# An expert phase dissolved into the attention heads around it, and the expert sums added in the last 20 heads

## The chip, the cores and the metric

One core of one Trainium2 chip. The metric is the device time of one execution in microseconds (us); the figure of a kernel is the median of its runs.

## The reference, cut to what matters

The input x is (4, 1024, 256). One layer norm feeds both an attention and a mixture of experts; both results are added to x.

```python
xn = _layernorm(x)                         # 4096 tokens, 256 columns
x = x + attention(xn) + moe(xn)
# attention: 16 heads of 128, causal softmax over 1024 tokens, @ Wo + bo
# moe:
shared = silu(g_s) * y_s @ w_shared_down   # y_s, g_s = split(xn @ w_shared_up)
scores = sigmoid(xn @ w_gate)              # 64 experts, top 6, weights normed
up  = einsum('ecd,edh->ech', x_disp, w_up) # x_disp: 128 token places an expert
g_r, v_r = split(up)                       # 32 hidden columns each
out_r = einsum('ech,ehd->ecd', silu(g_r) * v_r, w_down)
routed = (out_r[flat_e, pos_c] * w).sum(over the 6 chosen)
```

## The kernel before, in words

There are 64 heads: 4 batch rows times 16 heads, numbered 0 to 63 and worked one after the other. Each engine has its own order, written out by hand in a function `attention(i0, i1)` (one each for SP L401, POOL L530, PE L741, ACT L934 and DVE L1357), and semaphores tie the orders together. In a head, eight blocks of 128 query rows (j = 0 to 7) go through: PE `scores` (L697) into four PSUM banks; DVE `block_max` (L1307), which moves them to SBUF with the row maximum; ACT `softmax_exp` (L865) and `high_probs` (L870), POOL `low_probs` (L483), which split the exponentials into two f16 halves; SP `transpose_probs` (L387), a transposing DMA; and PE `values` (L712) and `project_y` (L727), one head behind the scores. `add_y` (L1330) on DVE adds a head's output to `resid`, the running sum. Queries, keys and values of the next head (`project_q`, `project_k`, `project_v`) are cut into the order between blocks; they and their readers `high_*` (ACT) and `low_*` (DVE) use the two banks of `ps_t`. `ps_y` holds the output of `project_y`. Block 0 to 7 of a head is also called slot 0 to 7 here.

The mixture of experts has four parts:

- Routing. In heads 0 to 32 the gates, the shared expert and the slots of the chosen experts are worked out, in even, odd and late parts of heads (`even_part`, `odd_part`, `late_part`). In heads 2 to 33 POOL scatters normed rows to a DRAM table `dispatched` with indirect DMAs (`scatter`, L511).
- Experts. After head 33 (`SPLIT` = 34) every engine leaves `attention`, with the last head's values and outputs finished and no new head begun. Then `experts(g, first)` runs 8 rounds of two groups of four experts (L806 on PE). A group loads 512 rows (`ex`), turns them to columns with 8 PE transposes (L816) into the score banks, which ACT (L1017) and DVE (L1475) copy to `exT`; runs 8 up projections (L826) of 64 columns; works out the silu with ACT (L1022) and four DVE instructions (L1480 to L1486); transposes the hidden rows (L832), which ACT copies (L1026); runs four down projections (L838) of 32 rows and 256 columns, each pair of halves of `eo` copied by ACT (L1034) and DVE; and stores `eo` to `expert_out` (L1040). All of it is f32. When all stores have landed, a new `attention(34, 64)` starts with its projections.
- Gathers. From head 34 on, POOL gathers one row tile per indirect DMA (`gather`, L522, called in L530's order after `low_probs`) into `got`: 32 token tiles times 6 choices. The order gives one step a slot, 7 steps to a token tile, of which 6 gather.
- Mixes. DVE `mix` (L1345) adds `got` times its weight to `resid` (L1352), and once a tile the constant `cvec` (L1355): 7 steps a tile, 224 in all, one a slot, 12 slots (`MIX_LAG`) behind the gathers, so 8 a head to slot 3 of head 63. `mix_at(j)` is called after block 1 for slots 0 and 1, between the two `low_q` for slot 2, after block 3 for slots 3 and 4, after block 5 for slots 5 and 6, and after block 7 for slot 7.

## Time and profile before

| | us |
|---|---|
| median of 3 runs (lowest, highest) | 1820.65 (1816.66, 1821.87) |
| profiled execution, its own time | 1822.72 |
| its span, first to last instruction | 1821.0 |
| PE busy | 1690.2 (93%) |
| DVE busy | 1368.7 (75%) |
| POOL busy | 1122.1 (62%) |
| ACT busy | 1085.7 (60%) |

Busy time is the union of an engine's instructions; PE's ends are modelled, so a busy PE can still run below its peak. PEclk is the clock that was granted to TensorE, as a share of 2.4 GHz. In the page's 40 slices of the span the four of the expert phase and of the stop around it (21 to 24) have PE busy 8, 6, 7 and 7 tenths and a granted clock of 9, 7, 6 and 6; in most others both have 9.

### The profile page before, as it was taken

How to read it: one execution, taken by the hardware profiler on the slowest of the kernel's cores; microseconds unless marked ns; L12 is line 12 of the kernel's file. 1: busy time of each engine (PE TensorE's matmuls, PEld its weight loads, DVE VectorE, ACT ScalarE, POOL GpSimd, SP SyncE). 2: the span in 40 equal slices, each digit the busy share in tenths (PEclk: the TensorE clock that was granted, in tenths of full speed). 3: DMA queues.
4: the chain of work that ended last, by engine and by line, in shares of the span. 5: the costliest groups of instructions: out<-in, count | busy, mean ns of one | idle time of the engine just before them, and what ended most of it. 6: DMA issues, size and time to landing. Idle time of an engine off the chain costs nothing. (4 is left out here: it accounts for less than half of the span.)

```text
span 1821.0 us, 49686 instructions
## 1 busy us (share of the span) xinstructions
PE 1690.2 (93%) x19217; PEld 1315.9 (72%) x19217; DVE 1368.7 (75%) x3128; ACT 1085.7 (60%) x2347; POOL 1122.1 (62%) x1006
## 2 busy tenths in 40 slices
PE   4699999999999999999986779999998999999997
PEld 3477767777777777777665667777776777777775
DVE  8677777777677777777663446888888888888885
ACT  2566666665566666666661227666666666666664
POOL 0257757776676777776660006777777677777763
PEclk7799999999999999999997669999999999999998
DMA  9377667765656665656656656778988789898976
GB/s 372 112 152 131 121 120 128 135 112 101 120 94 101 96 106 95 96 95 101 115 99 160 206 160 119 138 142 141 164 140 159 122 141 165 139 143 136 163 129 113
DMA packets 686658, 245.04 MB, mean 135 GB/s; under 512 B 637456, under 2 KB 674721, under 8 KB 685536
## 3 DMA queue, kind: packets, MB, share of 16 engines
q1 hardware_dynamic: 657472, 197.83, 61.6%
q0 software_dynamic: 18432, 33.64, 7.7%
q10 hardware_dynamic: 10528, 10.49, 1.8%
q8 instruction: 150, 2.46, 0.5%
q14 instruction: 76, 0.62, 0.1%
HBM read 57.11 MB, written 50.46 MB: 59 GB/s over the span
## 5 line engine op out<-in xcount | busy, mean ns | idle before, releaser
L485 POOL TENSOR_TENSOR prob<-prob 128x128 f16<-128x128 f32 (+7 forms) x512 | 653.0, 1280 | 576.1 <-ACT prob L874 569.2
L867 ACT ACTIVATE prob<-prob,nmax 128x128 f32<-128x128 f32 (+7 forms) x512 | 396.8, 775 | 530.4 <-DVE prob L1312 514.3
L708 PE MATMUL ps_s<-kT,qT 128*128 128x512 f16 (+3 forms) x2304 | 459.7, 327 | 4.3 <-DVE prob L1312 4.3
L723 PE MATMUL ps_o<-probT,vh 128*128 128x256 f16 (+1 forms) x3840 | 428.3, 265 | 7.2 <-DMA probT<-prob 7.2
L1312 DVE TENSOR_SCALAR_CACHE_REDUCE prob<-ps_s,neg_scale 128x128 f32<-128x128 f32 (+7 forms) x512 | 412.2, 809 | 14.3 <-PE ps_s L710 10.6
L723 PEld LDWEIGHTS ps_o<-probT,vh 128*128 128x128 f16 x3840 | 368.7, 99 | 53.5 <-issue 9.1
L874 ACT CAST prob<-prob 128x128 f16<-128x128 f32 (+7 forms) x512 | 341.5, 667 | 2.3
L708 PEld LDWEIGHTS ps_s<-kT,qT 128*128 128x128 f16 x2304 | 201.9, 98 | 144.7 <-issue 4.3
L1341 DVE SCALAR_TENSOR_TENSOR resid<-ps_y,yscale,resid 128x256 f32<-128x256 f32 x512 | 223.0, 477 | 11.6 <-PE ps_y L737 5.8
L737 PE MATMUL ps_y<-wo,oT 128*128 128x256 f16 x1536 | 210.6, 273 | 22.2 <-DVE oT L1327 20.4
L599 PEld LDWEIGHTS ps_t<-xT,wq 128*128 128x128 f16 x6144 | 205.1, 100 | 24.6 <-issue 9.8
L525 POOL DMA_INDIRECT got<-expert_out,slot_idx x192 | 201.1, 1048 | 32.6 <-issue 28.5
L599 PE MATMUL ps_t<-xT,wq 128*128 128x64 f16 x6144 | 214.3, 196 | 4.2 <-issue 2.3
L518 POOL DMA_INDIRECT dispatched<-xn,slot_idx x192 | 192.6, 1003 | 33.5 <-issue 33.0
L622 PE MATMUL ps_t<-xT,wk 128*128 128x512 f16 x768 | 189.2, 383 | 4.1 <-DVE qT L1293 4.0
L643 PE MATMUL ps_t<-wv,xT 128*128 128x128 f16 x3072 | 183.6, 220 | 9.6 <-DVE wv L1141 9.0
L1327 DVE SCALAR_TENSOR_TENSOR oT<-ps_o,oT 128x256 f16<-128x256 f32 x256 | 107.5, 420 | 109.6 <-ACT oT L898 106.0
L643 PEld LDWEIGHTS ps_t<-wv,xT 128*128 128x128 f16 x3072 | 175.7, 98 | 17.6 <-DVE wv L1141 9.3
L737 PEld LDWEIGHTS ps_y<-wo,oT 128*128 128x128 f16 x1536 | 138.7, 98 | 47.1 <-DVE oT L1327 27.2
L1299 DVE SCALAR_TENSOR_TENSOR kT<-ps_t,bkT,kT 128x512 f16<-128x512 f32 x128 | 95.8, 749 | 94.3 <-ACT kT L878 86.0
L1352 DVE SCALAR_TENSOR_TENSOR resid<-got,gate_w,resid 128x256 f32<-128x256 f32 x192 | 148.3, 772 | 3.2
L1293 DVE TENSOR_TENSOR qT<-ps_t,qT 128x512 f16<-128x512 f32 x128 | 87.8, 688 | 59.2 <-ACT qT L886 51.7
(182 smaller groups left out, 1651.6 us busy)
## 6 DMA issues: line engine op xcount, KB each, us to landing
dispatched<-zeros SPq DMA_DIRECT2D x16, 512.0 KB, 14.1
probT<-prob SPq DMA_TRANSPOSE x512
ex<-dispatched SPq DMA_DIRECT2D x16, 512.0 KB, 4.3
expert_out<-eo ACTq DMA_DIRECT2D x16, 512.0 KB, 3.7
eup<-in_L_ffn_w_up_dram SPq DMA_DIRECT2D x64, 64.0 KB, 2.1
dispatched<-xn,slot_idx POOLq DMA_INDIRECT x192
xn_columns<-xnth SPq DMA_DIRECT2D x24, 128.0 KB
got<-expert_out,slot_idx POOLq DMA_INDIRECT x192
```

The costliest lines, as they stand in the source:

```text
L485: pool.tensor_tensor(low_cols(j), prob_cols(j).rearrange("p (r k) -> p r k", k=P), high_cols(j), ALU.subtract).then_inc(p_low, 1)
L518: pool.indirect_dma_start(out=disp_d, out_offset=bass.IndirectOffsetOnAxis(ap=slot_idx[:, t, k:k + 1], axis=0), in_=xn[:, t // 2 % 3, t % ...
L525: pool.indirect_dma_start(out=got[:, t % 2, k, :], out_offset=None, in_=eout_d, in_offset=bass.IndirectOffsetOnAxis(ap=slot_idx[:, t, k:k ...
L599: mm = pe.matmul(ps_t[:, half, col:col + TPH], wq[:, a, k, m * D:(m + 1) * D], xT[:, c, k, h * TPH:(h + 1) * TPH], start=False, stop=(n + ...
L643: mm = pe.matmul(ps_t[:, half, r * D:(r + 1) * D], xT[:, a, k, tok:tok + P], wv[:, c, k, h * D:(h + 1) * D], start=(n + k == 0), stop=(n + ...
L708: pe.matmul(s_cols(j, lo, hi), qT[:, u, a, j * P:(j + 1) * P], kT[:, u, c, lo:hi], start=(n == 0), stop=(n == 2 and hi < w))
L723: mm = pe.matmul(ps_o[:, lo:2 * P], vh[:, u, a, r * D:(r + 1) * D], probT[:, PT_AT[c] + 2 * r + s, lo:], start=(r + n == 0), stop=(r == 2 ...
L737: mm = pe.matmul(ps_y[:, e * C:(e + 1) * C], oT[:, c % 2, a, e * P:(e + 1) * P], wo[:, s, h, :], start=(n == 0), stop=(n == 2))
L867: nc.scalar.activation(prob_cols(j), prob_cols(j), ACT.Exp, bias=nmax[:, j:j + 1], scale=-1.0, accum_out=rsum[:, i % 2, j:j + 1]).then_inc ...
L874: nc.scalar.copy(high_cols(j), prob_cols(j).rearrange("p (r k) -> p r k", k=P)).then_inc(p_high, 1)
L1312: V.tensor_scalar(prob_cols(j), s_cols(j, 0, (j + 1) * P), neg_scale[:], None, ALU.mult, ALU.min, accum_out=nmax[:, j:j + 1]).then_inc(s_m ...
L1341: ins = V.scalar_tensor_tensor(out=row, in0=ps_y[:, e * C:(e + 1) * C], scalar=yscale[:, j:j + 1], in1=row, op0=ALU.mult, op1=ALU.add)
```

## The change

The loop `experts` and the split of `attention` are gone; every engine runs heads 0 to 63 in one order. Head i of 35 to 42 is `early` for groups 2e and 2e+1 (e = i - 35): their rows are turned to columns and group 2e is projected up. Head i of 36 to 43 is `later` for groups 2e-2 and 2e-1 (e = i - 35): group 2e-1 is projected up, both are projected down, copied and stored. The four row blocks of a group go through `ps_t[0]` and `ps_y` in the place of the score banks; `exT`, `eup`, `edn` and `eo` are single instead of double. The hidden values are first copied from PSUM to SBUF (`eu`, ACT) and DVE reads them there. The down projection is two matmuls of 64 rows and 512 columns, with `edn` zero where the experts don't meet, in the place of four of 32 rows and 256 columns. The loads of rows move from SP to ACT, the stores are cut in two, and the loads of weights stay on SP, between the transposing DMAs. Gathers start in head 44 (`GA0`), after the last store has landed; mixes run at 12 a head (`MIXES`), 10 slots behind: one in slots 0, 2, 4 and 6 and two in slots 1, 3, 5 and 7, to slot 7 of head 63.

```diff
-        MIX_LAG = 12
+        MIX_LAG = 10
+        MIXES = 12
         NP = NT // 2
         ROWS = 2 * NP
-        SPLIT = ROWS + 2
+        NGR = E // EG
+        EX0 = ROWS + 3
+        GA0 = EX0 + NGR // 2 + 1
         GATES = E + 2 * HS
...
+        def early(i):
+            return i - EX0 if EX0 <= i < EX0 + NGR // 2 else -1
+
+        def later(i):
+            return i - EX0 if EX0 < i <= EX0 + NGR // 2 else -1
+
+        def gathers_by(s):
+            return max(0, min(NT * TOPK, s * MIXES * TOPK // (TB * (TOPK + 1))))
+
+        def mixes_by(s):
+            return max(0, min(NT * (TOPK + 1), (s - MIX_LAG) * MIXES // TB))
...
+            def load_up(n):
+                if n:
+                    sp.wait_ge(eu_done, n)
+                else:
+                    sp.wait_ge(ex_in[0], 16)
+                for e in range(EG):
+                    sp.dma_start(eup[:, e, :, :], w_up[n * EG + e].rearrange("(k p) n -> p k n", p=P)).then_inc(eup_in, 16)
+
+            def load_down(n):
+                if n:
+                    sp.wait_ge(ed_done, 2 * n)
+                else:
+                    sp.wait_ge(edn_zero, 1)
+                for e in range(EG):
+                    sp.dma_start(edn[e * HE:(e + 1) * HE, e % 2 * C:(e % 2 + 1) * C], w_down[n * EG + e]).then_inc(edn_in, 16)
...
-
-            attention(0, SPLIT)
-
-            for n in range(6):
-                sp.wait_ge(scattered[n], 16 * TOPK * len(range(n, NT, 6)))
-            sp.wait_ge(y_added, NC * SPLIT)
...
-            load_experts(0, True)
-            with sp.Fori(1, E // EG // 2) as g:
-                load_experts(g, False)
-            attention(SPLIT, B * H)
+                        if j == 0 and early(i) >= 0:
+                            load_up(2 * early(i))
+                        if j == 0 and later(i) >= 0:
+                            load_down(2 * later(i) - 2)
+                        if j == 3 and later(i) >= 0:
+                            load_down(2 * later(i) - 1)
+                        if j == 4 and early(i) >= 0:
+                            load_up(2 * early(i) + 1)
+
+            attention(0, B * H)
...
+            for i in range(B * H):
...
+                    if i == EX0 and j == 0:
+                        pool.wait_ge(ex_in[0], 16)
+                        pool.memset(edn[:], 0.0).then_inc(edn_zero, 1)
+                    s = TB * (i - GA0) + j
+                    for n in range(gathers_by(s), gathers_by(s + 1)):
+                        gather(n)
...
+            def rows_to_columns(i, n, h):
+                dst = ps_t[:, 0, :] if n % 2 + h == 0 else ps_y[:]
+                if n % 2 + h:
+                    pe.wait_ge(y_added, NC * (i - 1) + 2 * (n % 2) + h + 1)
+                elif turn(i, True):
+                    pe.wait_ge(v_low, 2 * i + 1)
+                else:
+                    pe.wait_ge(q_low, 2 * i + 3)
+                if h == 0:
+                    pe.wait_ge(ex_in[n % 2], 16 * (n // 2 + 1))
+                for e in range(2):
+                    for k in range(KC):
+                        mm = pe.transpose(dst[:, (2 * e + k) * P:(2 * e + k + 1) * P], ex[:, n % 2, 2 * h + e, k * P:(k + 1) * P], ident[:])
+                mm.then_inc(et_done, 1)
+
+            def up_project(i, n):
+                if n % 2:
+                    pe.wait_ge(y_added, NC * (i - 1) + 1)
+                elif n:
+                    pe.wait_ge(eo_d, n - 1)
+                else:
+                    free_bank(i, 1)
+                pe.wait_ge(eup_in, 16 * EG * (n + 1))
+                pe.wait_ge(eta_ready, n + 1)
+                pe.wait_ge(etd_ready, n + 1)
+                dst = ps_y[:, 2 * P:] if n % 2 else ps_t[:, 1, 2 * P:]
+                for e in range(EG):
+                    for k in range(KC):
+                        mm = pe.matmul(dst[:, e * 2 * HE:(e + 1) * 2 * HE], exT[:, e, k, :], eup[:, e, k, :],
+                                       start=(k == 0), stop=(k == KC - 1))
+                mm.then_inc(eu_done, 1)
+
+            def hidden_columns(i, n):
+                pe.wait_ge(eh_ready, n + 1)
+                if n % 2:
+                    pe.wait_ge(eo_d, n)
+                else:
+                    pe.wait_ge(y_added, NC * (i - 1) + 1)
+                dst = ps_t[:, 1, 0:P] if n % 2 else ps_y[:, 0:P]
+                pe.transpose(dst, eh.rearrange("p e h -> p (e h)"), ident[:]).then_inc(eht_done, 1)
+            def down_project(i, n, h):
+                bank = (n + h) % 2
+                if n % 2 == 0:
+                    free_bank(i, bank)
+                elif h == 0:
+                    pe.wait_ge(eu_taken, min(n + 2, NGR))
+                else:
+                    pe.wait_ge(k_low, 2 * (i + 1) + 1)
+                if h == 0:
+                    pe.wait_ge(edn_in, 16 * EG * (n + 1))
+                    pe.wait_ge(eht_ready, n + 1)
+                two = slice(2 * h * HE, 2 * (h + 1) * HE)
+                pe.matmul(ps_t[:, bank, :], ehT[two, n % 2, :], edn[two, :], start=True, stop=True).then_inc(ed_done, 1)
...
+                if c == 0 and early(i) >= 0:
+                    pe.wait_ge(etd_ready, 2 * early(i) + 2)
+                if c == 1 and later(i + 1) >= 0:
+                    pe.wait_ge(eht_ready, 2 * later(i + 1) - 1)
+                    pe.wait_ge(eu_taken, 2 * later(i + 1))
+                if c == 2 and early(i + 1) >= 0:
+                    pe.wait_ge(etd_ready, 2 * early(i + 1) + 1)
+                if c == 3 and early(i + 1) >= 0:
+                    pe.wait_ge(eta_ready, 2 * early(i + 1) + 2)
...
+                    if later(i) >= 0:
+                        hidden_columns(i, 2 * later(i) - 2)
+                        up_project(i, 2 * later(i) - 1)
...
+                    if early(i) >= 0:
+                        rows_to_columns(i, 2 * early(i), 0)
+                    if old:
                         values(i - 1, 2)
                     scores(i, 3)
+                    if early(i) >= 0:
+                        rows_to_columns(i, 2 * early(i), 1)
...
+                    if later(i) >= 0:
+                        down_project(i, 2 * later(i) - 2, 0)
+                        down_project(i, 2 * later(i) - 2, 1)
+                    if old:
...
+                    if later(i) >= 0:
+                        hidden_columns(i, 2 * later(i) - 1)
+                    if early(i) >= 0:
+                        up_project(i, 2 * early(i))
+                        rows_to_columns(i, 2 * early(i) + 1, 0)
...
+                    if later(i) >= 0:
+                        down_project(i, 2 * later(i) - 1, 0)
...
+                    if early(i) >= 0:
+                        rows_to_columns(i, 2 * early(i) + 1, 1)
+                    if later(i) >= 0:
+                        down_project(i, 2 * later(i) - 1, 1)
...
-            attention(0, SPLIT)
-            pe.wait_ge(y_added, NC * SPLIT)
-            def experts(g, first):
...
-            experts(0, True)
-            with pe.Fori(1, E // EG // 2) as g:
-                experts(g, False)
-            pe.wait_ge(eo_a, E // EG)
-            pe.wait_ge(eo_d, E // EG)
-            attention(SPLIT, B * H)
+            attention(0, B * H)
...
+            def load_expert_rows(n):
...
+                    act.wait_ge(et_done, 2 * n - 2)
+                act.dma_start(ex[:, n % 2, :, :], rows_v[n]).then_inc(ex_in[n % 2], 16)
...
+            def first_columns(n):
+                act.wait_ge(et_done, 2 * n + 1)
+                if n:
+                    act.wait_ge(eu_done, n)
+                nc.scalar.copy(exT[:, 0:2, :, :].rearrange("p e k s -> p (e k s)"), ps_y[:] if n % 2 else ps_t[:, 0, :]).then_inc(eta_ready, 1)
+            def take_hidden(n):
+                act.wait_ge(eu_done, n + 1)
...
+                src = ps_y[:, 2 * P:] if n % 2 else ps_t[:, 1, 2 * P:]
+                nc.scalar.copy(eu[:].rearrange("p e n -> p (e n)"), src).then_inc(eu_taken, 1)
+            def gate_of_hidden(n):
+                act.wait_ge(eu_taken, n + 1)
+                nc.scalar.activation(eg, eu[:, :, 0:HE], ACT.Exp, scale=-1.0).then_inc(eg_exp, 1)
+            def copy_hidden(n):
+                act.wait_ge(eht_done, n + 1)
...
+                src = ps_t[:, 1, 0:P] if n % 2 else ps_y[:, 0:P]
+                nc.scalar.copy(ehT[:, n % 2, :], src).then_inc(eht_ready, 1)
+            def first_outputs(n):
+                act.wait_ge(ed_done, 2 * n + 1)
...
+                nc.scalar.copy(eo[:, 0:2, :].rearrange("p e c -> p (e c)"), ps_t[:, n % 2, :]).then_inc(eo_a, 1)
+
+            def store_outputs(n, h):
+                act.wait_ge(eo_d if h else eo_a, n + 1)
+                act.dma_start(outs_v[n][:, 2 * h:2 * h + 2, :], eo[:, 2 * h:2 * h + 2, :]).then_inc(eo_out[h], 16)
...
+            def second_columns(n):
...
+                V.tensor_copy(exT[:, 2:4, :, :].rearrange("p e k s -> p (e k s)"), ps_y[:]).then_inc(etd_ready, 1)
+
+            def hidden(n):
+                dve.wait_ge(eg_exp, n + 1)
+                V.tensor_scalar(eg, eg, 1.0, None, ALU.add).then_inc(eh_step, 1)
...
+                V.reciprocal(eh, eg).then_inc(eh_step, 1)
...
+                V.tensor_tensor(eg, eu[:, :, 0:HE], eh, ALU.mult).then_inc(eh_step, 1)
+                dve.wait_ge(eh_step, 3 * n + 3)
+                V.tensor_tensor(eh, eu[:, :, HE:], eg, ALU.mult).then_inc(eh_ready, 1)
+            def second_outputs(n):
+                dve.wait_ge(ed_done, 2 * n + 2)
...
+                V.tensor_copy(eo[:, 2:4, :].rearrange("p e c -> p (e c)"), ps_t[:, (n + 1) % 2, :]).then_inc(eo_d, 1)
...
                     def mix_at(j):
-                        n = TB * (i - i0) + j - MIX_LAG
-                        if mixing and 0 <= n < NT * (TOPK + 1):
+                        s = TB * (i - GA0) + j
+                        for n in range(mixes_by(s), mixes_by(s + 1)):
                             mix(n // (TOPK + 1), n % (TOPK + 1), NC * (i - 1) + (1, 1, 1, 2, 2, 3, 3, 4)[j])
...
+                    if later(i) >= 0:
+                        hidden(2 * later(i) - 1)
+                    if i == EX0 - 1:
+                        gate_weights()
...
+                    if early(i) >= 0:
+                        second_columns(2 * early(i))
...
+                    if later(i) >= 0:
+                        second_outputs(2 * later(i) - 2)
...
+                    if early(i) >= 0:
+                        hidden(2 * early(i))
...
+                    if early(i) >= 0:
+                        second_columns(2 * early(i) + 1)
+                    if later(i) >= 0:
+                        second_outputs(2 * later(i) - 1)
                     mix_at(7)
...
-            attention(0, SPLIT, False)
...
```

## Rows read from the trace of the kernel before

**Rows 1.** ACT timeline (start, duration): first exponential of heads 36, 45, 46.
```profile
1138.69 0.40 ACT L867 ACTIVATE prob<-prob,nmax 128x128 f32<-128x128 f32 x1
...
1350.65 0.40 ACT L867 ACTIVATE prob<-prob,nmax 128x128 f32<-128x128 f32 x1
...
1374.22 0.40 ACT L867 ACTIVATE prob<-prob,nmax 128x128 f32<-128x128 f32 x1
```

**Rows 2.** stretches: length, busy us by engine, clock, DMA share, GB/s.
```profile
931.80:1138.70 206.90, 164.85 (x1411) 135.19 (x1412) 102.50 (x224) 75.62 (x169) 51.22 (x45) 0.78 0.63 154
...
1061.00:1074.00 13.00, 9.68 (x66) 8.41 (x66) 6.25 (x13) 3.43 (x8) 0.00 (x0) 0.76 0.74 221
...
1350.60:1374.20 23.60, 23.53 (x294) 18.37 (x291) 20.44 (x46) 15.81 (x35) 17.66 (x16) 1.00 0.88 141
...
1256.60:1280.20 23.60, 23.50 (x293) 18.35 (x290) 21.20 (x46) 15.70 (x35) 16.60 (x15) 1.00 0.91 135
```

**Rows 3.** one stretch, row transposes (L816) alone.
```profile
1061.00:1074.00 13.00, 3.42 (x16) 3.21 (x16) 0.76 0.74 221
```

**Rows 4.** two stretches, up projection (L826) alone.
```profile
1028.00:1041.00 13.00, 6.93 (x32) 6.95 (x32) 0.50 0.70 208
...
1061.00:1074.00 13.00, 3.68 (x32) 3.65 (x32) 0.76 0.74 221
```

**Rows 5.** PE timeline, down projections of one round (two groups).
```profile
1025.57 0.71 PE L838 MATMUL ps_s<-edn,ehT 32*128 32x256 f32 x8 [0.45 <-ACT ehT L1026]
...
1026.29 0.41 PE L838 MATMUL ps_t<-edn,ehT 32*128 32x256 f32 x2
```

**Rows 6.** DVE timeline, head 45; in brackets idle time and releaser.
```profile
1350.23 0.74 DVE L1299 SCALAR_TENSOR_TENSOR kT<-ps_t,bkT,kT 128x512 f16<-128x512 f32 x1
...
1351.43 0.88 DVE L1341 SCALAR_TENSOR_TENSOR resid<-ps_y,yscale,resid 128x256 f32<-128x256 f32 x2
...
1354.18 0.69 DVE L1293 TENSOR_TENSOR qT<-ps_t,qT 128x512 f16<-128x512 f32 x1 [0.21 <-issue]
...
1360.66 1.29 DVE L1305 TENSOR_TENSOR vh<-ps_t,vh 128x512 f16<-128x512 f32 x2 [0.43 <-ACT vh L891]
...
1367.39 0.75 DVE L1299 SCALAR_TENSOR_TENSOR kT<-ps_t,bkT,kT 128x512 f16<-128x512 f32 x1 [0.45 <-issue]
...
1369.13 0.87 DVE L1341 SCALAR_TENSOR_TENSOR resid<-ps_y,yscale,resid 128x256 f32<-128x256 f32 x2
...
1371.45 2.16 DVE L1355 TENSOR_TENSOR resid<-resid,cvec 128x256 f32<-128x256 f32 x1
```

**Rows 7.** PE timeline, head 45: two query projections, a mask, last values.
```profile
1349.62 0.38 PE L592 MATMUL ps_t<-bq_pick,bq_rows 128*128 128x512 f16 x1
...
1351.48 0.38 PE L592 MATMUL ps_t<-bq_pick,bq_rows 128*128 128x512 f16 x1
...
1369.43 0.22 PE L710 MATMUL ps_s<-causal,identb 128*128 128x128 bf16 x1
...
1384.57 1.69 PE L723 MATMUL ps_o<-probT,vh 128*128 128x256 f16 x14
```

**Rows 8.** waits, 1327 to 1397 us: total us, times, longest.
```profile
ACT oT L898 <- PE ps_o L723: 0.8, 3, 0.3
...
DVE prob L1312 <- PE ps_s L710: 0.6, 3, 0.2
```

**Rows 9.** by line, ns min/median/max: the mix, the gather.
```profile
L1352 DVE SCALAR_TENSOR_TENSOR resid<-got,gate_w,resid x192: 474/485/2162, 1124.0 to 1786.2; 128x256 f32<-128x256 f32 x192
...
L525 POOL DMA_INDIRECT got<-expert_out,slot_idx x192: 1015/1022/1268, 1098.1 to 1758.5; - x192
```

**Rows 10.** SP, loads of weights of one group in the old loop.
```profile
1055.08 2.07 SPq L437 DMA_DIRECT2D eup<-in_L_ffn_w_up_dram  x4
```

**Rows 11.** POOL timeline, head 45.
```profile
1371.44 1.88 POOL L485 TENSOR_TENSOR prob<-prob 128x896 f16<-128x896 f32 x1 [0.46 <-ACT prob L874]
```

**Rows 12.** DVE timeline, head 63.
```profile
1792.53 1.29 DVE L1305 TENSOR_TENSOR vh<-ps_t,vh 128x512 f16<-128x512 f32 x2 [1.01 <-ACT vh L891]
```

More of the change, by code:

```diff
@@ L243, in causal_attention_with_moe @@
         ex_in = [sem(f"ex_in{u}") for u in range(2)]
-        eup_in = [sem(f"eup_in{u}") for u in range(2)]
-        edn_in = [sem(f"edn_in{u}") for u in range(2)]
+        eup_in = sem("eup_in")
+        edn_zero = sem("edn_zero")
+        eu_taken = sem("eu_taken")
+        edn_in = sem("edn_in")
         et_done = sem("et_done")
@@ L257, in causal_attention_with_moe @@
         eo_d = sem("eo_d")
-        eo_stored = sem("eo_stored")
+        eo_out = [sem(f"eo_out{h}") for h in range(2)]
         gathered = [sem(f"gathered{u}") for u in range(2)]
@@ L520, in scatter, with gather @@
                     in_=xn[:, t // 2 % 3, t % 2, :], in_offset=None, bounds_check=SLOTS - 1, oob_is_err=False).then_inc(scattered[t % 6], 16)
-            def gather(t, k):
+            def gather(n):
+                t, k = divmod(n, TOPK)
+                if n == 0:
+                    for h in range(2):
+                        pool.wait_ge(eo_out[h], 16 * NGR)
                 if t > 1:
@@ L619, in project_k @@
                     pe.wait_ge(base_step, 2 * odd_part(i - 1) + 2)
+                if later(i - 1) >= 0:
+                    pe.wait_ge(eo_a, 2 * later(i - 1) - 1 + half)
+                elif early(i - 1) >= 0 and half == 1:
+                    pe.wait_ge(eu_taken, 1)
                 for n, (a, c) in enumerate(PASSES):
@@ L627, in project_v @@
                 h = i % H
+                if half == 0 and early(i) >= 0 and not turn(i, more):
+                    pe.wait_ge(eta_ready, 2 * early(i) + 1)
                 if i == 0 and half == 0:
@@ L635, in project_v @@
                         pe.wait_ge(bd_added, odd_part(i - 1) + 1)
+                    if half == 0 and later(i - 1) >= 0:
+                        pe.wait_ge(eo_d, 2 * later(i - 1))
                     if half == 0 and even_part(i - 1) >= 0:
@@ L1432, in attention @@
                         add_y(i - 1, 2, mixed(4))
+                    if later(i) >= 0:
+                        second_outputs(2 * later(i) - 2)
+                    if old:
                         low_o(i - 1, 3)
```

288 lines of the change are left out of this document (116 added, 172 removed).

## The prediction

> **What bounds the kernel now.** Four views, in this order. The stretches of the span come first [rows 2]: in a plain head of the mixing part PE is busy 23.53 of 23.60 us at a granted clock of 1.00, DVE 20.44, POOL 17.66, ACT 15.81. From the first exponential of one head to that of the next is 23.57 us [rows 1], and I call this the pitch. PE sets it. The same view shows the exception: from 931.80 to 1138.70, heads 33, 34 and 35 with the expert loop between them, three heads took 206.9 us at a mean clock of 0.78 [rows 1, 2]. There the engines wait for one another: in a round of 13.0 us PE is busy 9.68, DVE 6.25 and ACT 3.43 [rows 2]. The timeline of DVE and the waits say how far behind PE the others are in a plain head. DVE and ACT together wait for PE only (0.8 + 0.6) / 3 = 0.47 us a head [rows 8]; DVE's other idle time is spent waiting for ACT, which in turn had waited for DVE [rows 6]. So the DVE-ACT loop is about 23.1 us long beside PE's 23.57. PE is the bound, and this loop is the next one, by half a microsecond.
>
> **What goes.** Three heads at the pitch are 3 x 23.6 = 70.8 us. The stop and the loop cost 206.9 - 70.8 = 136.1 us beyond them: the drain after head 33, eight rounds of 13.0 us and more, and the refill.
>
> **PE work that comes back.** PE has no spare time in a plain head, so each expert instruction is paid in full, at full clock. A pair of groups (one head's worth) needs 16 row transposes, 3.42 us [rows 3], and 32 up-projection instructions, 3.68 us [rows 4]. Its two hidden transposes, at 3.42 / 16 each, are 0.4 us. The down projections change shape. Before, eight matmuls of 256 columns ran four abreast, in two rounds from 1025.57 to 1026.70, so 0.57 us a round with the drain [rows 5]. Now there are four of 512 columns with 64 rows, so at most two abreast. 512 columns cost between 0.85 (estimate: two rounds by 0.57 less the overlap of the drain) and 1.14. The even group's two stand together and the odd group's apart: three times 0.9 is 2.7 us; 1.7 if both run abreast, 4.6 if none does. Sum 3.42 + 3.68 + 0.4 + 2.7 = 10.2 us a pair, between 9.2 and 12.1. Eight pairs: **+82 us** (74 to 97).
>
> **The other engines in heads 35 to 43.** These heads have no mixes, and the pitch there becomes 23.6 + 10.2 = 33.8 us. DVE loses its mixes (seven of about half a microsecond and one of 2.16 [rows 6, 9]) and gains 6.25 us a pair, ACT gains 3.43 [rows 2], a PSUM copy a group and six DMA issues of about half a microsecond, as SP's [rows 10]: both stay far below 33.8. I cost this work at nothing; PE's longer head hides it. SP gets 16 weight loads a head of 0.5 us each (four take 2.07) [rows 10] between the transposing DMAs. POOL's last-but-one block is ready at 1371.44 + 1.88 = 1373.3 and the values that read it start at 1384.57 [rows 7, 11], so four or eight loads ahead of a transpose fit in. One wait is new on POOL: its first gather, in head 44, waits until ACT's last store, issued after `softmax_exp(44, 1)`, has landed, and `low_probs` of the next blocks are queued behind it. That is once, some 4 us, and the same 11 us to the values cover it.
>
> What is late is order, at two places. `rows_to_columns` of the odd group's second half stands right after the last scores and waits for `add_y` of the head before, part 3. In head 45 that ends at 1369.13 + 0.87 = 1370.0, the scores at 1369.43 + 0.22 [rows 6, 7]: 0.35 late already, and now `hidden` (four dependent DVE instructions) stands ahead of it on DVE. `hidden_columns` after `scores(i, 1)` waits for `add_y` part 0, which ends at 1352.31, while PE goes on at 1349.62 [rows 6, 7]: 2.7 us late, but 1.7 of it come from the 2.16 us mix ahead of it, which these heads don't have. Behind each stands the whole PE queue. The lower end is nothing; the upper end is that all waiting of the old round comes back, 13.0 - 9.68 = 3.3 us [rows 2]. I take 1.8 us, 0.8 for `hidden` and 1.0 for the rest, since both places show about a microsecond: **+14 us** for 8 heads (0 to 26).
>
> **The mixes packed into heads 45 to 63.** Twelve a head where there were eight, one more in each of the four places (after blocks 1, 3, 5 and 7). A mix takes 0.485 us in the middle [rows 9], so four are 1.94 us of DVE. Three of the places are followed by an idle wait, 0.21, 0.43 and 0.45 us [rows 6], which the mix fills: 1.94 - 1.09 = 0.85 us more loop. The 0.47 us before PE's pitch would take part of it. But POOL is in it too: it gathers 10.3 instead of 6.9 times a head, 3.4 x 1.02 = 3.5 us more, 21.2 of 23.6, with the DMA engines at 0.88 already [rows 2], and what it does late, DVE's `block_max` and the transposes get late. Lower end nothing, as PE is not relieved; upper end 1.94 - 0.47 and one more mix that meets a POOL subtraction like the one of slot 7, 2.16 - 0.485 = 1.67 more, so 3.1. I take 0.8, near the sum of the rows: 19 heads, **+15 us** (0 to 59).
>
> The mix of slot 7 starts at 1371.45, with the POOL subtraction at 1371.44, and ends at 1373.6, when POOL's 1.88 us are over [rows 6, 11]. The Trainium skill's SBUF page ("SBUF — State Buffer", the section "SBUF: two separate sides") has the rule: a VectorE instruction with two SBUF inputs and a GpSimd one that reads SBUF share a port pair by an exclusive lock held for the whole instruction. The trace agrees, 2.16 against 0.485 us. By it the second mix of a place mostly costs its bare time, since it stands behind the first; but `hidden`, whose two products now read `eu` and `eh` in SBUF rather than PSUM, can be locked out in heads 35 to 43: an estimate by the rule is one subtraction of 1.88 us a pair that reaches PE in full, 8 x 1.9 = 15 us, and a median of 1812. Without the rule nothing is added for it, and the sum above goes that way.
>
> **The end.** Head 63 had 4 mixes and gets 12; 1.01 us of idle [rows 12] and others take some; the pair ahead of `block_max` 6 doesn't hide. **+1.5 us** (0 to 5).
>
> **Sum.** -136.1 + 82 + 14 + 15 + 1.5 = -23.6 us. The profiled execution took 1822.7 us (span 1821.0 and 1.7 around it), so the changed one would take 1799.1; the median of the runs stands 2.1 below the profiled one, which makes **1797 us**.
>
> **Rivals.**
> - *All but PE's work is hidden* (both stalls and the mixing cost nothing): -136.1 + 82 = -54, 1766.6 us. For it: in the head at 1256.6 DVE was busy 21.20, 0.8 more, at the same 23.6 pitch [rows 2]. Against: one such head can live on a reserve, nineteen can't, and the places above.
> - *DVE becomes the bound of the last 20 heads, and it is slower than before.* Each head's added mixes meet POOL's subtractions at two more places for a full 1.67 us: 1.94 + 3.34 - 0.47 = 4.8 us a head, 91 us; with the other terms -136.1 + 82 + 14 + 91 + 1.5 = +52, 1873 us. It decides from (136.1 - 97.5) / 19 = 2.0 us a head on, the point of no gain. For it: POOL subtracts in a good part of each head and slot 7 does meet it. Against: a place has one first mix, and three of the four places had one before. At 2.4 us a head, its mild form, 1828.
> - *The expert work in the heads stalls PE as the loop did* (3.3 us a head and 12.1 us of work): -136.1 + 97 + 26 + 15 + 1.5 = +3.4... with the mixing at nothing -12, so 1809 to 1824.
> - *The clock falls in heads 35 to 43.* The same 32 up-projection instructions took 6.93 us at a clock of 0.50 (1.2 GHz) and 3.68 in a round granted 0.76 on average [rows 4]; that fall came after PE had waited some 3 us in each round. If a stall of 1 to 2 us a head brought stretches at 0.50, then a fifth of nine heads of 34 us at half speed costs 30 us: 1827 us. Against: plain heads are granted 1.00 with PE busy 99% [rows 2].
> - *The change doesn't do what it says:* no way for that; PE's expert instructions are all still there, only the waiting goes.
>
> **How the numbers follow.** Forecast 0.60 (own range 1784 to 1812); all hidden 0.20; stalls of the loop's size 0.08; mixing bound, slower 0.08; clock 0.04. The range for 8 in 10 goes from all hidden, 1766, to 1820, between the forecast's end and the stalls. 0.3%, 5.5 us, is about what a measurement of this kernel can tell from no change. Faster: 0.60 + 0.20 + 0.06 of the stalls = 0.86; same: 0.02 of the stalls, 0.02 of the mixing's mild form and 0.01 of the clock, 0.05; slower: 0.06 + 0.03 = 0.09.
>
> **What would show it.** No stretch of the changed profile has PE under 9 tenths but the start, the end and the turns of a batch row; the clock stays near 1.00 from 900 to the end. Heads 36 to 42 take 35 to 36 us, with PE 95% busy and idle before the row transposes of the odd group and the hidden transposes; the f32 instructions on PE add up to 80 us. Heads 45 to 62 take 24.4 us, with DVE 95% busy and small PE idle times released by DVE. If their pitch is 23.6 the step on the mixes was wrong; if over 25.6, or if PE idles over 3 us a head behind expert work, the forecast is.

## The result and the profile after

The changed kernel takes 1830.93 us in the median of four runs (1826.02 to 1833.38), the kernel before 1819.89 on the same chip (1816.66 to 1821.87): a ratio of 1.0059, 95% interval 1.0033 to 1.0085. It is slower, by 0.6%: a small loss, with the whole interval above 1. The forecast was 1797 us. The profiled execution took 1826.0 us (span 1824.3), 3.3 more than the one before.

Three stretches hold nearly all of it: heads 33 to 35, 36 to 44 and 45 to 62, each from a first exponential to a first exponential. Behind them stand two expert heads (36 and 37) and the cheapest and the dearest plain head of the mixing part (48 and 58).

```profile
core 0: us, PE busy (x) PEld busy (x) DVE busy (x) ACT busy (x) POOL busy (x), PEclk, DMA share, GB/s
929.40:1008.30 78.90, 73.84 (x866) 57.45 (x863) 51.72 (x123) 49.45 (x109) 38.34 (x33) 1.00 0.68 118
1008.30:1326.20 317.90, 290.77 (x3040) 216.89 (x3038) 184.68 (x424) 174.15 (x384) 99.70 (x80) 0.98 0.67 137
1326.20:1786.20 460.00, 430.93 (x5128) 331.55 (x5124) 414.51 (x879) 284.56 (x614) 375.84 (x330) 0.99 0.90 156
1008.30:1045.00 36.70, 32.61 (x341) 24.04 (x339) 21.60 (x50) 19.91 (x46) 10.18 (x8) 1.00 0.66 139
1045.00:1083.30 38.30, 34.70 (x346) 26.07 (x344) 21.57 (x50) 19.99 (x46) 10.19 (x8) 0.96 0.73 138
1406.40:1430.80 24.40, 24.34 (x305) 18.83 (x301) 22.41 (x50) 15.71 (x34) 20.72 (x19) 1.00 0.87 152
1659.30:1686.10 26.80, 23.87 (x246) 17.87 (x247) 24.45 (x50) 15.71 (x34) 20.74 (x19) 0.95 0.83 139
```

| stretch (us) | before | after | difference |
|---|---|---|---|
| start to head 33 | 931.8 | 929.4 | -2.4 |
| heads 33 to 35 | 206.9 | 78.9 | -128.0 |
| heads 36 to 44 | 211.9 | 317.9 | +106.0 |
| heads 45 to 62 | 432.1 | 460.0 | +27.9 |
| head 63 and the end | 38.3 | 38.1 | -0.2 |

The stop went as worked out [rows 2]: against three heads at the old pitch, 136.2 us. But the twelve heads from 33 to 44 together take 396.8 us, 114.0 more than 12 x 23.57, where 96 stood in the sum; and the last heads cost 28 where 15 stood.

**Why the expert heads are long.** The waits of heads 37 and 38, then PE and DVE in head 37 (start, duration, what, and in brackets the idle time before it with its releaser):

```profile
PEld ps_y L701 <- DVE resid L1464: 7.3, 4, 2.6
PE ps_y L701 <- DVE resid L1464: 6.0, 4, 2.3
...
PE ps_y L728 <- DVE resid L1464: 1.2, 2, 0.6
```

```profile
1055.16 0.81 PE L799 MATMUL ps_s<-kT,qT 128*128 128x512 f16 x3
1055.81 0.22 PE L801 MATMUL ps_s<-causal,identb 128*128 128x128 bf16 x1
1058.33 0.91 PE L701 MATMUL ps_y<-ident,ex 128*128 128x128 f32 x4 [2.30 <-DVE resid L1464]
1059.03 2.23 PE L676 MATMUL ps_t<-wv,xT 128*128 128x128 f16 x19
```

```profile
1053.15 0.22 DVE L1500 TENSOR_SCALAR w_gs<-w_gs 128x128 f32<-128x128 f32 x1
1053.40 0.95 DVE L1504 RECIPROCAL w_gs<-w_gs 128x128 f32<-128x128 f32 x1
1054.38 0.29 DVE L1506 TENSOR_TENSOR w_gs<-eu,w_gs 128x128 f32<-128x128 f32 x1
1054.71 0.29 DVE L1508 TENSOR_TENSOR w_gs<-eu,w_gs 128x128 f32<-128x128 f32 x1
1054.92 0.61 DVE L1435 TENSOR_SCALAR_CACHE_REDUCE prob<-ps_s,neg_scale 128x384 f32<-128x384 f32 x1
...
1057.07 0.42 DVE L1450 SCALAR_TENSOR_TENSOR oT<-ps_o,oT 128x256 f16<-128x256 f32 x1 [1.53 <-ACT oT L972]
1057.41 0.87 DVE L1464 SCALAR_TENSOR_TENSOR resid<-ps_y,yscale,resid 128x256 f32<-128x256 f32 x2
```

And ACT in the same stretch:

```profile
1055.57 0.61 ACT L941 ACTIVATE prob<-prob,nmax 128x384 f32<-128x384 f32 x1 [2.86 <-DVE prob L1435]
...
1056.19 0.56 ACT L1030 COPY exT<-ps_t 128x512 f32<-128x512 f32 x1
1056.65 0.38 ACT L972 ACTIVATE oT<-ps_o 128x256 f16<-128x256 f32 x1
```

`hidden` of the odd group (four instructions, 1.84 us from 1053.15, whose buffers the profile calls w_gs) stands ahead of block_max 2, low_o and add_y part 1 of the head before. It reaches add_y by way of ACT: the exponential of block 2 waits for block_max 2, ACT copies oT only behind it and behind an expert copy (`exT`, 0.56 us), and low_o waits 1.53 us for that. The add_y frees ps_y, and the row transposes of the even group's second half need ps_y: PE waits 2.30 us. The other row transposes wait 0.70, the hidden transpose 0.60, so 3.6 us a pair. In all, heads 35 to 43 (978.7 to 1301.2) have 30.9 us of PE's waits, nearly all of them for add_y:

```profile
PE ps_y L701 <- DVE resid L1464: 23.9, 16, 2.3
PE ps_y L728 <- DVE resid L1464: 5.3, 8, 1.1
```

After the long wait, in heads 37, 39 and 41, the granted clock falls to half:

```profile
1056.20:1058.60 2.40, 0.27 (x2) 0.27 (x3) 1.53 (x4) 1.24 (x4) 0.91 (x1) 1.00 0.77 159
1058.60:1062.00 3.40, 3.40 (x32) 3.34 (x31) 1.03 (x3) 0.98 (x3) 0.00 (x0) 0.50 0.32 63
```

0.50 is the level of 1.2 GHz, and it makes these heads 1.6 us longer than their neighbours. PE's expert instructions themselves, each group of them counted to the start of the next instruction, come to 9.26 us a pair in the timeline of head 37, less than the 10.2 of the sum.

**Why the mixing heads are long.** In DVE's column: 22.4 to 24.5 us busy where one head before had 20.44 [rows 2]. POOL is busy 20.7 instead of 17.66, and its waits for ACT shrank from 4.8 us in one head before (1350.6 to 1374.2) to 1.8 in one after (1351.7 to 1376.5). DVE's mix instructions in heads 48 to 58 (x count | busy, mean ns | idle before):

```profile
L1475 DVE SCALAR_TENSOR_TENSOR resid<-got,gate_w,resid 128x256 f32<-128x256 f32 x113 | 84.4, 747 | 3.5 <-issue 0.4
L1478 DVE TENSOR_TENSOR resid<-resid,cvec 128x256 f32<-128x256 f32 x19 | 15.8, 834 | 0.3
```

Before, the same heads had 76 mixes at a mean of 801 ns, of which 0.485 is the bare time [rows 9]. So the twelve mixes are not each dearer; there are more of them. With the additions of `cvec` they take 9.1 us of DVE a head instead of 6.2, 2.9 more, where the sum took four bare ones, 1.94. Of the twelve, 2.5 a head last over 1 us and 1.2 of these 1.8 or more; before it was 1.5 and 1.1 of eight.

PE was idle 0.02 us a head in heads 48 to 58 before and is idle 1.5 now. More than half of that is one wait, ahead of the query projection: DVE has the mixes of slot 7 in front of `low_k`, and PE waits for `low_k`. Before and after, 11 heads each:

```profile
PE ps_t L592 <- DVE kT L1299: 0.2, 1, 0.2
```

```profile
PE ps_t L617 <- DVE kT L1422: 9.3, 10, 1.4
```

### The profile page after: what moved, and what is told of

Same layout as the page of the kernel before. It is cut to its first block and busy times, and to the rows that moved or that the text cites. A ratio compares the mean times of both kernels' runs of the same rounds, so it can differ in the third digit from the quotient of the medians.

```text
span 1824.3 us, 49365 instructions
## 1 busy us (share of the span) xinstructions
PE 1679.8 (92%) x19153; PEld 1288.0 (71%) x19153; DVE 1363.1 (75%) x3120; ACT 1092.7 (60%) x2363; POOL 1122.2 (62%) x1007
## 5 line engine op out<-in xcount | busy, mean ns | idle before, releaser
L814 PE MATMUL ps_o<-probT,vh 128*128 128x256 f16 (+1 forms) x3840 | 422.5, 263 | 5.2 <-DMA probT<-prob 5.0
L814 PEld LDWEIGHTS ps_o<-probT,vh 128*128 128x128 f16 x3840 | 364.9, 98 | 55.2 <-issue 14.0
L549 POOL DMA_INDIRECT got<-expert_out,slot_idx x192 | 197.3, 1027 | 47.4 <-issue 34.2
L624 PEld LDWEIGHTS ps_t<-xT,wq 128*128 128x128 f16 x6144 | 201.4, 99 | 25.1 <-issue 9.9
L624 PE MATMUL ps_t<-xT,wq 128*128 128x64 f16 x6144 | 209.2, 194 | 5.5 <-issue 5.3
L676 PE MATMUL ps_t<-wv,xT 128*128 128x128 f16 x3072 | 189.5, 223 | 10.9 <-DVE wv L1264 8.7
L676 PEld LDWEIGHTS ps_t<-wv,xT 128*128 128x128 f16 x3072 | 181.4, 100 | 18.8 <-DVE wv L1264 9.1
L837 PEld LDWEIGHTS ps_y<-wo,oT 128*128 128x128 f16 x1536 | 137.8, 98 | 54.2 <-DVE oT L1450 27.9
L1475 DVE SCALAR_TENSOR_TENSOR resid<-got,gate_w,resid 128x256 f32<-128x256 f32 x192 | 139.9, 728 | 5.2 <-issue 0.4
## 6 DMA issues: line engine op xcount, KB each, us to landing
xn_columns<-xnth SPq DMA_DIRECT2D x24, 128.0 KB
```

The source lines that it names most:

```text
L549: pool.indirect_dma_start(out=got[:, t % 2, k, :], out_offset=None, in_=eout_d, in_offset=bass.IndirectOffsetOnAxis(ap=slot_idx[:, t, k:k ...
L624: mm = pe.matmul(ps_t[:, half, col:col + TPH], wq[:, a, k, m * D:(m + 1) * D], xT[:, c, k, h * TPH:(h + 1) * TPH], start=False, stop=(n + ...
L676: mm = pe.matmul(ps_t[:, half, r * D:(r + 1) * D], xT[:, a, k, tok:tok + P], wv[:, c, k, h * D:(h + 1) * D], start=(n + k == 0), stop=(n + ...
L814: mm = pe.matmul(ps_o[:, lo:2 * P], vh[:, u, a, r * D:(r + 1) * D], probT[:, PT_AT[c] + 2 * r + s, lo:], start=(r + n == 0), stop=(r == 2 ...
L837: mm = pe.matmul(ps_y[:, e * C:(e + 1) * C], oT[:, c % 2, a, e * P:(e + 1) * P], wo[:, s, h, :], start=(n == 0), stop=(n == 2))
```

## The experiments

"Pitch" is the mean of heads 48 to 58 of the profiled execution, 23.57 us before and 25.43 after. "Expert stretch" is heads 36 to 44, 317.9 us after. Every ratio is to the kernel before on the same chip, where its median was 1815.4 to 1820.0.

**1. Each part of the change alone.** `e6` leaves the expert work out (the gathers read the dispatched rows, so the sums are not the reference's):

```diff
-            return i - EX0 if EX0 <= i < EX0 + NGR // 2 else -1
+            return -1          # and the same in later(i)
```

> The changed kernel with the expert groups left out of heads 35 to 43 (no row transposes, projections, silu, copies, stores; gathers read the dispatch table instead, so the output lacks the experts); mixes and gathers as in the changed kernel. In the changed kernel heads 33 to 44 took 396.8 us where twelve heads at 23.57 would be 282.8, so theory A (the expert work and its stalls in the heads cost 114 us, everything else is where it was) expects the span to fall from 1824 to about 1712 and the mixing heads to stay at 25.3 us. Rival B (what slows heads 45 to 63 is something that the expert stage leaves behind, such as a DVE that has fallen back, or DMA traffic) expects the mixing heads at 23.6 and about 1680.

1710.65 us, ratio 0.9413 (0.9391 to 0.9435). Heads 36 to 43 at 23.3 us; pitch 25.23, heads 45 to 62 458.7 us. The loss of the mixing heads does not come from the expert heads.

`e5` packs eight mixes a head as before, and only 19 of 32 tiles are mixed at all (the rest of the output lacks its expert sums):

```diff
-        MIXES = 12
+        MIXES = 8
+        NTM = 19               # in place of NT in gathers_by, mixes_by
```

> The changed kernel with 8 mixes a head in heads 45 to 63 instead of 12, gathers in proportion; only the first 19 of 32 token tiles get their expert sums (the others are left out). Theory A (the packing of the mixes costs 1.6 us a head from head 45 on) expects the heads back at 23.6 us and the total down by 18 x 1.6 = 29 us, to about 1800. Rival B (these heads are slow for a reason other than the number of mixes, for instance the single edn, eo buffers' traffic or the new stores' split) expects 25.3 us a head still.

1795.86 us, 0.9879 (0.9855 to 0.9904), pitch 23.54, heads 45 to 62 428.9 us. The pace of twelve, of mixes and gathers together, is the whole of the mixing heads' loss.

**2. Length or gathers.** `e3` mixes 16 of the 256 columns (the other columns stay without sums), `e4` makes one of the six gathers of a tile and mixes its rows six times:

```diff
# e3
-    out=resid[:, t, :], in0=got[:, t % 2, k, :]
+    out=resid[:, t, 0:16], in0=got[:, t % 2, k, 0:16]
# e4, in gather(n)
+                if k:
+                    return
```

> The changed kernel with every mix cut to 16 of its 256 columns (240 columns of the expert sum are left out); all waits, gathers and the order stay. Theory A1 (the heads are slow because of DVE's own length and because mixes are locked out behind POOL's subtractions): DVE loses 12 x 0.24 us, but a mix that meets a subtraction of POOL still waits for its end, 1.6 us in slot 7 and 0.6 in slot 5. If length counts, 23.6 to 23.9 us a head and about 1798; if the lock is most of it, 24.5 or more. Rival C (the gathers on POOL and on the DMA engines slow the heads) expects 25.3 us as before.

> The changed kernel with one gather a token tile instead of six; all six mixes of a tile read that one (so the sums are of one expert row, five of six gathers left out). Mixes stay at 12 a head. Theory A1 (DVE's length and the lock) expects little: POOL is freer and its subtractions a bit earlier, 24.9 to 25.3 us a head. Rival C (POOL's 21 us of work a head, 3.5 more than before, and the DMA engines at 0.95) expects 23.6 to 23.8 us and about 1798.

`e3`: 1817.77 us, 0.9996 (0.9978 to 1.0013), pitch 24.77. `e4`: 1811.16 us, 0.9965 (0.9950 to 0.9980), pitch 24.36. The stretch of heads 48 to 58 in before, `e3` and `e4`:

```profile
1427.90:1687.16 259.26, 258.25 (x3152) 201.56 (x3149) 228.53 (x496) 173.18 (x375) 191.15 (x164) 1.00 0.88 144
```

```profile
1404.68:1677.15 272.47, 261.70 (x3172) 202.25 (x3168) 232.13 (x540) 173.30 (x376) 227.77 (x202) 1.00 1.00 159
```

```profile
1402.78:1670.70 267.92, 259.90 (x3165) 202.12 (x3161) 246.10 (x540) 173.17 (x374) 132.93 (x108) 1.00 0.69 116
```

`e3` gives DVE nearly its old work back (232.1 to 228.5 us), and 1.2 us of the pitch stay. `e4` gives POOL more than its old room, and 0.8 us stay. The two add up to 2.0, near the 1.86 lost. One part is DVE's length, 0.8 as forecast; the other comes with the gathers and was not in the sum. PE's wait for `low_k`, 9.3 us in 11 heads of the changed kernel, parts in the same way: `e3` ends most of it, and `e4`, whose PE is idle 7.6 us in all, keeps it.

```profile
PE ps_t L617 <- DVE kT L1422: 1.7, 4, 0.9
```

```profile
PE ps_t L619 <- DVE kT L1424: 7.2, 10, 0.8
```

**3. The place of `hidden`.** `e8` moves the odd group's behind add_y part 1, `e1` moves the even group's too, from before block_max 6 to after block_max 7:

```diff
# e8 and e1
-                    if later(i) >= 0:
-                        hidden(2 * later(i) - 1)      # ahead of block_max(i, 2)
                     ...
                         add_y(i - 1, 1, mixed(2))
+                    if later(i) >= 0:
+                        hidden(2 * later(i) - 1)
# e1 only
-                        hidden(2 * early(i))          # ahead of block_max(i, 6)
                         second_columns(2 * early(i) + 1)
+                        hidden(2 * early(i))
```

> The changed kernel with both `hidden` calls moved on DVE: the odd group's from before block_max 2 to after add_y part 1 of the head before, the even group's from before block_max 6 to after block_max 7. Theory A (the expert heads are too long because `hidden` stands ahead of block_max and add_y on DVE, and PE's row transposes wait 2.3 and 0.7 us a pair for the ps_y banks that add_y frees, after which the clock falls to 0.50 for 3.4 us in three of the heads): heads 36 to 42 drop from 37.5 to some 34.5 us, no stretch of them at 0.50, the stretch of heads 36 to 44 falls from 318 to about 295 us, the time to about 1807 us, ratio 0.987. Rival (the wait belongs to the expert work as such: the PSUM banks and the four dependent steps of `hidden` are late wherever they stand): the same 3 us turn up at the hidden transpose or the down projection, the stretch stays within 5 us of 318, the time at 1826 to 1833.

> As the one before, but only the odd group's `hidden` is moved behind add_y part 1; the even group's stays before block_max 6. Theory A: the 2.3 us wait before the even group's second row transposes of the next pair goes, and with it the fall of the clock; the 0.7 us wait before the odd group's stays. Heads 36 to 42 about 35.3 us, the time about 1812 us. Rival (both moves are needed, since the clock's fall hangs on the later wait too): heads of 36.5 us and more, 1820 us or over.

`e8`: 1823.04 us, 1.0028 (1.0014 to 1.0043); its expert heads take 35.75 us each and the stretch 307.1, 10.8 less than after, at a clock of 1.00. `e1`: 1850.38 us, 1.0178 (1.0147 to 1.0208), stretch 333.6. The stretch of `e8`, then the waits of two of its heads and of `e1`'s:

```profile
1008.50:1315.70 307.20, 288.55 (x3041) 214.19 (x3040) 184.22 (x424) 173.53 (x384) 99.71 (x80) 1.00 0.70 142
```

```profile
PE ps_y L701 <- DVE resid L1464: 3.4, 4, 1.0
...
PE ps_y L728 <- DVE resid L1464: 1.8, 3, 0.6
```

```profile
PE ps_y L728 <- DVE resid L1464: 5.0, 2, 2.5
...
PE ps_y L701 <- DVE resid L1464: 2.0, 2, 1.0
```

The odd group's place was a cause of the long stretch: the longest wait falls from 2.3 to 1.0 us and the fall of the clock is gone. In the total it does not show as clearly, since the intervals of `e8` and of the changed kernel overlap. My expectation of `e1` was wrong, by the same mechanism: late, the even group's `hidden` stands ahead of the next head's add_y part 0, which the hidden transpose (L728) needs. That wait grows from 0.6 to 2.5 us, and the stretch from 1010 to 1310 is granted 0.93.

**4. The place of the mixes.** `e2` lays them by slot as 2, 2, 2, 2, 2, 1, 1, 0; `e7` is `e2` with `e1`. The next four stand on `e8`: `e9` has 1, 1, 1, 1, 2, 2, 2, 2, `e12` has 2, 1, 2, 1, 2, 1, 2, 1, `e10` moves slot 7's mixes behind the next head's low_k, `e11` moves them ahead of block_max 7.

```diff
# e2, in mixes_by
-            (s - MIX_LAG) * MIXES // TB
+            s // TB * MIXES + (0, 2, 4, 6, 8, 10, 11, 12)[s % TB] - 16
# e11
+                    mix_at(7)
                     block_max(i, 7)
-                    mix_at(7)
```

> The changed kernel with the twelve mixes of a head laid by slot as 2, 2, 2, 2, 2, 1, 1, 0 instead of 1 or 2 in every slot, so that none follows block_max 7, where POOL subtracts. Theory A (the first mix of slot 7, 2.0 us instead of 0.48, is held by POOL's subtraction and is 1.5 us of the DVE-ACT loop): the pitch of heads 45 to 62 falls from 25.3 to 24.3 us, the time to about 1812 us. Rival (the lock goes where the mixes go, and what bounds these heads is the DVE, POOL and DMA work as a whole): another slot's first mix grows to 1.5 us or more, the pitch stays at 25.0 or above, the time at 1826 or above.

> Both moves of `hidden` and the slots of the mixes at once. Theory A on both: 1826 - 23 - 18 = about 1788 us, faster than the kernel before by 1.7%. Rival on the mixes with A on `hidden`: about 1806. Both rivals: 1826 or more.

> The odd group's `hidden` late, as in e8, and the twelve mixes by slot as 1, 1, 1, 1, 2, 2, 2, 2: pairs behind the long blocks. Theory B (what bounds the mixing heads is the DVE work between two exponentials together with POOL's subtractions, which lock DVE out; where PE's blocks are longest there is most room): a pitch of 25.0 us, the time about 1817 us. Rival C (the place matters by which mixes meet a subtraction; POOL's are longest behind the long blocks): first mixes of 2 us in slots 5 to 7, a pitch of 26 us or more, 1835 us.

> As e8, with the mixes of slot 7 moved behind the next head's block_max 0 and low_k half 1, so that the project_q of the head does not wait for them. Theory B (the loop as a whole is too long): the 1 us wait before project_q goes from PE's rows but comes back before the output projection or the scores, pitch 25.0 to 25.5 us, time 1820 us. Rival D (only the order is wrong: the locked mix stands ahead of low_k, for which PE waits): pitch 24.4 us, time about 1806 us.

> As e8, with the mixes of slot 7 ahead of block_max 7, where POOL is at a gather and does not subtract. Theory D (lock and order are what costs): the first mix of slot 7 falls from 2.0 to 0.5 us, pitch 24.3 us, time about 1805 us. Theory B: block_max 7, the cast and the subtractions behind it are later by the same amount, the pitch stays at 25 to 25.5 us, time 1820 us.

> As e8, with the mixes by slot as 2, 1, 2, 1, 2, 1, 2, 1: one instead of two behind blocks 1, 3, 5 and 7. Theory B: pitch unchanged, 25 to 25.5 us, time 1820 us. Theory D (slot 7's second mix stands ahead of low_k and slot 0's does not): 0.7 us a head less, pitch 24.7 us, time about 1811 us.

| | ratio (95%) | pitch | DVE busy a head |
|---|---|---|---|
| after | 1.0059 (1.0033 to 1.0085) | 25.43 | 23.4 |
| e8 | 1.0028 (1.0014 to 1.0043) | 25.47 | 23.4 |
| e2 | 1.0125 (1.0104 to 1.0146) | 25.98 | 22.3 |
| e7 | 1.0221 (1.0200 to 1.0243) | 26.08 | 22.2 |
| e9 | 1.0054 (1.0039 to 1.0069) | 26.00 | 23.4 |
| e10 | 1.0131 (1.0102 to 1.0159) | 26.59 | 22.9 |
| e11 | 1.0043 (1.0026 to 1.0060) | 25.93 | 21.9 |
| e12 | 1.0030 (1.0012 to 1.0049) | 25.66 | 23.2 |

No order has a shorter pitch than the changed kernel's own; theory A on the slots fell in `e2`, theory D in `e10`, `e11` and `e12`, and `e9` came out at the pitch of its rival C. In `e10` PE's wait ahead of the query projection is gone, but PE now waits 12.8 us in 11 heads for low_o and 4.9 for add_y, ahead of the output projection: the place of a mix moves the wait. `e11` did what it was made for, its mixes last 627 ns in the mean instead of 748, and DVE stands idle 4.1 us a head instead of 2.0 (pitch less busy time).

**5. Bytes, lock or buffer.** All stand on `e8`. `e13` stores and gathers the expert rows as f16, `e14` gathers 16 of the 256 columns, which the mix reads sixteen times over (sums not the reference's), `e15` is `e13` with `e11`'s order.

```diff
# e13
-    eout_d = nc.dram_tensor("expert_out", (SLOTS + P, C), F32, kind="Internal").ap()
+    eout_d = nc.dram_tensor("expert_out", (SLOTS + P, C), F16, kind="Internal").ap()
     ...                    # and the views of eo and got as F16
# e14
-    out=got[:, t % 2, k, :], in_=eout_d
+    out=got[:, t % 2, k, 0:16], in_=eout_d.rearrange("r (a c) -> (r a) c", c=16)
```

> As e8, with the expert outputs stored and gathered as f16: the same gathers and mixes, half the bytes of each row. Theory DMA (at a share of 0.95 the gathers hold up the transposing transfers of the probabilities, and POOL and ACT with them): DMA share falls to about 0.85, the pitch to 24.4 us, near that with one gather of six, the time to about 1806 us. Theory POOL (a gather's 1.02 us on POOL and its order with the subtractions is the price): pitch unchanged at 25.2 to 25.7, time 1820 to 1823.

> As e8, but each gather brings 16 of the 256 columns of a row (the mix reads them sixteen times over), so the sums are not the reference's; instructions and their number stay on POOL and DVE. Theory DMA: pitch 24.3 us as with few gathers, time about 1804. Theory POOL: pitch 25.2 us or more, time over 1818.

> As e13, with the mixes of slot 7 ahead of block_max 7. If the lock adds its price once the DMA engines are relieved, 24.0 us of pitch and about 1798 us; if not, the same as e13 within 3 us.

`e13`: 1816.76 us, 1.0009 (0.9996 to 1.0021), pitch 25.28. `e14`: 1816.32, 1.0005 (0.9993 to 1.0017), pitch 25.37. `e15`: 1817.91, 1.0016 (1.0003 to 1.0029), pitch 25.34. Heads 48 to 58 of `e14` and of `e15`:

```profile
1397.14:1676.17 279.03, 261.65 (x3117) 201.19 (x3114) 257.22 (x540) 172.78 (x375) 229.46 (x202) 0.99 0.68 106
```

```profile
1396.90:1675.68 278.78, 262.13 (x3135) 201.35 (x3136) 239.10 (x540) 172.47 (x375) 229.28 (x202) 0.99 0.88 129
```

A DMA share of 0.68 in `e14` instead of 0.95 in `e8`, and the same pitch: it is not the bytes. `e15` has DVE at 239.1, 7 us less than `e4` had with its pitch of 24.36, and still takes 25.34: it is not DVE's busy time with the lock in it either. What `e4` had and none of these has is POOL's time, 132.9 instead of 229 us.

At twelve mixes a head two tiles pass in 9.3 slots, and the mixes stand 10 slots behind the gathers; so a gather can stand ahead of the mix that frees its buffer, and POOL waits for DVE 8.8 us in heads 45 to 62, which it never did before. `e16` sets the lag to 7, `e17` also slows the pace to 11.75, `e18` (on `e13`) has four half-size buffers.

```diff
# e16
-        MIX_LAG = 10
+        MIX_LAG = 7
# e18
-                    pool.wait_ge(mix_step, (TOPK + 1) * (t - 2) + k + 1)
+                    pool.wait_ge(mix_step, (TOPK + 1) * (t - 4) + k + 1)
```

> As e8, with the mixes 7 slots behind the gathers instead of 10. A tile's two buffers pass in 9.3 slots at this pace, so with 10 a gather stands ahead of the mix that frees its buffer and POOL waits for DVE (13 times, 8.8 us in heads 45 to 62), with 7 never. Theory buffer (POOL's wait for the mix ties POOL to DVE and is the second microsecond): those waits gone, pitch 24.4 us, heads 45 to 62 at 440 us, time about 1803 us. Theory length (10.3 gathers of 1.02 us and 0.16 between them make POOL's own loop too long): waits gone, pitch still 25 us or more, time within 4 us of e8, 1819 to 1827.

> As e16, at 11.75 mixes a head instead of 12, which the shorter lag leaves room for. Either theory: 0 to 3 us below e16.

> As e13 (rows as f16), with four gather buffers in the memory of the two, so that a gather waits for a mix four tiles back. Theory buffer: POOL's waits for mixes (9 to 14 us in heads 45 to 62) are gone and so is what they hold up, pitch 24.4 us, time about 1801 us. Theory length: waits gone, POOL waits that much longer for ACT instead, pitch 25.0 to 25.5 us, time 1813 to 1819, as e13.

`e16`: 1860.96 us, 1.0248 (1.0224 to 1.0272), pitch 28.25; `e17`: 1852.30, 1.0198 (1.0177 to 1.0219), 8.7 us below `e16` where 0 to 3 were expected, pitch 27.43. POOL's waits for mixes are gone, but DVE now waits for the rows (`e16`, 1330 to 1770 us), which neither theory foresaw:

```profile
DVE resid L1475 <- DMA got<-expert_out,slot_idx: 39.0, 18, 4.0
```

`e18`: 1820.76 us, 1.0005 (0.9990 to 1.0019), pitch 25.24. One wait of POOL for a mix is left, of 0.3 us, none of DVE for the rows, and the pitch stays. The buffers' wait was not the price.

What stays with the gathers is that POOL comes late. From the end of ACT's cast of a block to the start of POOL's subtraction, summed over the eight blocks of a head (heads 48 to 58, from the timelines), pass 4.7 us before, 8.9 in the changed kernel, in `e8` and in `e14`, 8.1 in `e18`, 10.8 in `e3` and 2.5 in `e4`. This points to the length of POOL's own order, 10.3 gathers of 1.02 us with 0.16 between, but it is argued by elimination and not shown: `e4` takes away the number of transfers together with POOL's time, and no run parts the two.

No version with the reference's sums was faster than the kernel before. The nearest are `e13` and `e18`, level with it.

## Why the prediction was wrong

- *What bounds, and what goes:* right. -136.1 forecast, 136.2 read off.
- *PE's expert work, +82:* right in kind, 9.26 us a pair, +74. In head 37 the row transposes came to 2.2 us where the row gave 3.42, the up projections to 3.5 for 3.68; the down projections to 3.2 for 2.7, for the even group's two took 1.07 us abreast and each of the odd group's 1.05 alone, all near the upper end of 0.85 to 1.14.
- *The order, +14:* this is the first step that failed; it measured 40. The two places named were there, at 0.70 and 0.60 us where 1.8 was taken for both. The third was missed: I looked at `hidden` only ahead of the odd group's transposes, and never asked what stands behind the other `hidden` on DVE. It delays add_y part 1, and PE waits 2.3 us a pair. PE's waits in heads 35 to 43 are 30.9 us. With the 4.9 us of the three clock falls and the edge heads 34 and 44 (25.4 and 25.0 us where the pitch was 23.6), all beyond PE's work is 40 us. `e8` shows 10.8 of it to be the place of that one call. One of the prediction's own signs of being wrong came with it: PE idles over 3 us a head behind expert work.
- *Nothing for the clock in heads 35 to 43:* right in sign as a rival, far smaller (4.9 us for 30).
- *The mixes, +15:* the second; they measured 28. DVE's length cost 0.8 a head (`e4`), near the 0.85 worked out, in part by luck: the four mixes took 2.9 us of DVE and not 1.94. But the sum put nothing for POOL's added 3.5 us, since POOL had 2.4 us left in 23.6. What goes with the gathers cost another 1.0 to 1.2 a head (`e3`, `e4`). That it is the length of POOL's order, which needs this room for its waits for ACT, is argued and not shown.
- *The end, +1.5:* -0.2.

Together, in profiled time: -136.2 + 114.0 + 27.9 - 0.2 and -2.4 at the start, +3.1; the span grew by 3.3, for heads 36 to 44 took 0.2 less than nine pitches before. The rest of the difference is the medians': the profiled execution after is the quickest of its four, 4.9 below their median, where the one before stood 2.8 above.

Two rivals each came half true, the stalls "as the loop did" (3.6 us of waits a pair for 3.3) and the mild form of the mixing bound (1.55 a head for 2.4). I gave them 0.16 together, and no case in which both came. That the first one's sum, +3.4, is the measured +3.3 is luck: its work was 97 where 74 came, its stalls 26 for 40, its mixes 15 for 28.

By the Trainium skill ("SBUF — State Buffer", "SBUF: two separate sides") a VectorE instruction with two SBUF inputs and a GpSimd one that reads SBUF lock each other out for a whole instruction. The traces agree: all 40 mixes of the changed kernel that last over 1 us end 0.29 us after a POOL subtraction, and a mix of 16 columns still took 579 ns in the mean in `e3`. As a price it misled: `e11` and `e15` took much of it away and gained nothing. The 15 us that the prediction estimated by the rule for `hidden` are not there either: its first product lasted 0.29 to 0.65 us, its second 0.29.

## What to carry to other kernels

When work is inserted in an engine's order, write down for each inserted call the next instruction behind it whose end another engine waits for, and do it for every place it is put; the costliest place here was the one not written down, and the repair of `e1` made the same mistake one place further on. When a pace is raised by half, check the room of every engine in the loop and not the fullest alone, and the buffers' distance in slots against the lag; the room that an engine seems to have may be its wait for the others.
